# Decoder layer on one core: the second attention's queries and both output projections as three fp32r products, and the feature transposes on halves of 64 rows

## The reference

```
x = x + attn(layernorm(x))            # 16 heads of 16: softmax features of k and q (64 per head), then a linear attention
x = x + xattn(layernorm(x), ctx)      # 8 heads of 32 over 77 context rows of width 192
x = x + ffn(layernorm(x))             # 8 causal heads of 64, values and outputs by one of 8 experts per head and token

xattn:  q = x @ Wq + bq ; w = softmax(q k^T / sqrt(32)) ; out = (w v) @ Wo + bo
attn:   ... num/den per head ... ; out = ctx @ Wo.T + bo
```

## Time and profile before

| what | value |
|---|---|
| median of 3 runs | 913.57 us (910.67 to 914.4) |
| the profiled execution | 910.57 us, its span 907.6 us |
| granted PE clock | 0.998 of full speed over the span |
| PE busy | 853.4 us (94%) |
| DVE busy | 609.5 us (67%) |
| ACT busy | 310.1 us (34%) |
| POOL busy | 319.6 us (35%) |

### The profile page before, as it was taken

One profiled execution on the slowest core, in us unless ns is written; L12 is line 12 of the kernel. 1 busy time (PEld: TensorE's weight loads), 2 busy tenths in 40 slices (PEclk: granted clock), 3 DMA queues, 4 the chain that ended last, 5 costly groups with the idle time before them and its releaser, 6 DMA issues.

```text
span 907.6 us, 17162 instructions
## 1 busy us (share of the span) xinstructions
PE 853.4 (94%) x6944; PEld 648.0 (71%) x6944; DVE 609.5 (67%) x894; ACT 310.1 (34%) x510; POOL 319.6 (35%) x307
## 2 busy tenths in 40 slices
PE   5979899999999998989999888999999999998998
PEld 3657678877756543889976675888777556458998
DVE  4767566566555466888868674765764555687887
ACT  3637655210055554111034475641002444440000
POOL 5213312221457888367520032200004745771000
PEclk9999999999999999999999999999999999999999
DMA  8104000424224553255540000012122010316562
GB/s 274 43 26 140 2 1 1 145 74 138 70 70 143 168 193 96 81 190 177 170 139 1 3 3 1 1 55 77 64 92 93 2 26 2 72 45 192 183 193 87
DMA packets 46789, 80.15 MB, mean 88 GB/s; under 512 B 13064, under 2 KB 24104, under 8 KB 46712
## 3 DMA queue, kind: packets, MB, share of 16 engines
q1 hardware_dynamic: 46711, 79.07, 28.3%
HBM read 59.55 MB, written 19.33 MB: 87 GB/s over the span
## 4 chain that ended last, share of the span: by engine, by line
PE 81%; POOL 6%; DVE 5%; ACT 3%; DMA 3%; issue 2%; SPq 0%; POOLq 0%; DVEq 0%; ACTq 0%
PE ps L1238 19%; PE ps L1643 11%; PE ps L1565 6%; PE ps L1649 5%; PE ps L1476 5%; PE ps L1537 5%; PE ps L1246 5%; POOL xT L610 4%; PE ps L1423 3%; PE ps L1500 3%; PE ps L1380 3%; PE ps L1397 3%; PE ps L1280 2%; PE ps L1317 2%; PE ps L1438 2%
## 5 line engine op out<-in xcount | busy, mean ns | idle before, releaser
L610 POOL TENSOR_TENSOR xT<-xT,region 128x1024 f32<-128x1024 f32 (+5 forms) x80 | 129.7, 1622 | 71.1 <-PE ps L1565 65.9
L1643 PE MATMUL ps<-expert_hi,k_hi 128*128 128x256 f32 x512 | 124.6, 283 | 4.6 <-DVE k_hi L1137 4.6
L1153 DVE COPY_PREDICATED region<-region,ps 128x512 f32<-128x512 uint32 x112 | 82.3, 735 | 66.7 <-PE ps L1238 66.0
L1643 PE MATMUL ps<-expert_lo,k_hi 128*128 128x256 f32 x512 | 123.1, 279 | 0.0
L1077 DVE TENSOR_REDUCE region<-ps 128x2 f32<-128x1024 f32 (+2 forms) x96 | 89.1, 954 | 46.2 <-PE ps L1510 25.3
L1238 PE MATMUL ps<-expert_hi,wide_hi 128*128 128x512 f32 x256 | 102.4, 400 | 0.0
L1643 PEld LDWEIGHTS ps<-expert_hi,k_hi 128*128 128x128 f32 x512 | 96.0, 188 | 6.0 <-issue 4.8
L1238 PE MATMUL ps<-expert_hi,wide_lo 128*128 128x512 f32 x256 | 100.0, 391 | 0.0
L1238 PE MATMUL ps<-expert_lo,wide_hi 128*128 128x512 f32 x256 | 99.8, 390 | 0.0
L1643 PEld LDWEIGHTS ps<-expert_lo,k_hi 128*128 128x128 f32 x512 | 96.7, 189 | 0.0
L1137 DVE TENSOR_TENSOR k_hi<-region 128x1024 fp32r<-128x1024 f32 x64 | 81.9, 1280 | 17.1 <-issue 16.8
(11 more groups left out here) (161 smaller groups left out, 1641.5 us busy)
## 6 DMA issues: line engine op xcount, KB each, us to landing
region<-hot_rows SPq DMA_DIRECT2D x128, 128.0 KB, 3.3
expert_hi<-halves_kept SPq DMA_DIRECT2D x22, 384.0 KB, 3.3
expert_lo<-halves_kept SPq DMA_DIRECT2D x22, 384.0 KB, 4.3
halves_kept<-expert_hi SPq DMA_DIRECT2D x16, 512.0 KB, 5.4
halves_kept<-expert_lo SPq DMA_DIRECT2D x16, 512.0 KB, 6.2
expert<-in_value_experts SPq DMA_DIRECT2D x8, 512.0 KB, 4.6
expert<-in_output_experts SPq DMA_DIRECT2D x8, 512.0 KB, 4.4
gb<-scale_rows SPq DMA_DIRECT2D x16, 256.0 KB, 4.0
```

The costliest lines, as they stand in the source:

```text
L610: pool.tensor_tensor(acc(c)[:, heads, lo:CH], acc(c)[:, heads, lo:CH], PT[:, k % RING, heads, lo:CH], ALU.add).then_inc(sem["added"], 1)
L1153: dve.copy_predicated(V3[:, t].rearrange("p (h k) -> p h k", k=HD3), chosen.unsqueeze(2).broadcast_to([P, H3, HD3]), ps[:, n % 4, :].rearr ...
L1643: mm(ps[:, 4 + t // 2, t % 2 * D:(t % 2 + 1) * D], k_hi[n % 2][:, t * P:(t + 1) * P], w[:, slot, columns], start=(n == 0 and t % 2 == 0 an ...
```

## The change

- **Splits of the weights.** In the key stage of each batch, ACT rounds the three weights WoT, W2q and W2o to their high halves (after the exponentials of tiles 2, 3 and 5), and POOL subtracts to get the low halves, ahead of the maximum over the partitions. The halves lie in buffers of the feed-forward stage that are free until then (q_hi, k_hi, k_lo).
- **Output projections.** ACT's copy of `cx` transposed now writes the high half `cxT_hi`. DVE subtracts it from PSUM for the low half `cxT_low`, as its first work of each step, and PE makes y from six fp32r products instead of two fp32 ones. What waited for ACT's copy of bank 4 (`cxT_sb`) now waits for `cxT_low`: y, the next transpose of `cx`, and `sums_turned`, which writes to bank 4 as well.
- **Queries.** The normalised rows of a = 0 go to `wide_hi` (by ACT) and `wide_lo` (by DVE, `row_low`) and no longer to `xT`, and each of the four query products per batch is six fp32r products of 512 columns instead of two in fp32. `row_low` stands near the start of the step after the tile was transposed, for the last tile of each four at the end of the same step.
- **Feature transposes.** Each block of 128 x 128 is transposed as two halves of 64 tokens, on the upper and on the lower 64 rows of PE, into two different banks. ACT's copies put them back in order.

The diff, cut to its core:

```diff
@@ -179,6 +178,10 @@
                                   for n in ("k_hi", "k_lo", "q_hi", "q_lo"))
+        W2q_hl, WoT_hl, W2o_hl = (w[0][:, :].rearrange("p (w a n) -> p w a n", w=2, a=DA) for w in (q_hi, k_hi, k_lo))
+        cxT_hi, cxT_lo = (k_hi[1][:, i * 2 * D:(i + 1) * 2 * D].rearrange("p (i a s) -> p i a s", i=2, a=DA)
+                          for i in range(2))
+        SPLITS = ((W2q, W2q_hl), (WoT, WoT_hl), (W2o, W2o_hl))
         o_lo = lambda p: (wide_hi, wide_lo)[p // 2][:, p % 2, :]
...
@@ -267,6 +270,7 @@
         QUERIES_AT = {3: (0,), 4: (1,), 7: (2, 3)}
+        SPLIT_AT = {2: 0, 3: 1, 5: 2}
         OFFSET = (0, 10)
@@ -569,6 +573,10 @@
                         pool.wait_ge(w3_lo, i + 1)
+                for i, (w, halved) in enumerate(SPLITS):
+                    until(pool, "split_hi", b, i + 1)
+                    pool.tensor_tensor(halved[:, 1], w[:, :, :], halved[:, 0].bitcast(fp32),
+                                       ALU.subtract).then_inc(sem["split_lo"], 1)
                 until(pool, "ak_top_ready", b, 1)
@@ -644,6 +652,10 @@
                 until(act, "xnT_ps", b, a * TT + t + 1)
+                if a == 1:
+                    copy(wide_hi[:, :, t * P:(t + 1) * P],
+                         ps[:, row_bank(b, a, t), 0:D].rearrange("p (a s) -> p a s", a=DA), "xT_ready")
+                    return
@@ -702,6 +714,13 @@
                     act.activation(E1[:, t, :], E1[:, t, :], ACT.Exp).then_inc(sem["e_ready"], 1)
+                    if t in SPLIT_AT:
+                        w, halved = SPLITS[SPLIT_AT[t]]
+                        if b == 0:
+                            act.wait_ge(later_in, 16 * LOADS_LATER)
+                        else:
+                            until(act, "mo_used", b - 1, NEP)
+                        copy(halved[:, 0], w[:, :, :], "split_hi")
                     for n in queries[1:]:
@@ -741,11 +760,13 @@
                         i = t % 2
+                        turned = phT[:, i, :].rearrange("p (k i s) -> p i k s", i=2, s=HALF)
+                        halves = ps[:, 0:2, :].rearrange("p i (k s) -> p i k s", s=HALF)
                         if a == 0:
-                            copy(phT[:, i, :], ps[:, 0:2, :].rearrange("p a s -> p (a s)"), "fT_sb")
+                            copy(turned, halves, "fT_sb")
                         else:
-                            act.activation(phT[:, i, 0:CH], ps[:, 0, :], ACT.Copy)
-                            copy(phT[0:K2L, i, CH:CH + P], ps[0:K2L, 1, 0:P], "fT_sb")
+                            act.activation(turned[:, :, 0:K2C - 1], halves[:, :, 0:K2C - 1], ACT.Copy)
+                            copy(turned[0:K2L, :, K2C - 1], halves[0:K2L, :, K2C - 1], "fT_sb")
                     for a, t in due(s, 0):
@@ -753,7 +774,7 @@
                             until(act, "y_ps", b, a * TT + t - 1)
-                        copy(cxT[:, t % 2, :, :], ps[:, 4, 0:D].rearrange("p (a s) -> p a s", a=DA), "cxT_sb")
+                        copy(cxT_hi[:, t % 2], ps[:, 4, 0:D].rearrange("p (a s) -> p a s", a=DA), "cxT_sb")
                     for a, t in due(s, 6):
@@ -973,12 +994,27 @@
                                       ALU.mult).then_inc(sem["wv_ready"], 1)
+                def row_low(t):
+
+                    cs = slice(t * P, (t + 1) * P)
+                    until(dve, "xT_ready", b, TT + t + 1)
+                    dve.tensor_tensor(wide_lo[:, :, cs],
+                                      ps[:, row_bank(b, 1, t), 0:D].rearrange("p (a s) -> p a s", a=DA),
+                                      wide_hi[:, :, cs].bitcast(fp32), ALU.subtract).then_inc(sem["x_lo"], 1)
+
...
                 for s in range(LAST):
+                    for a, t in due(s, 4):
+                        until(dve, "cxT_sb", b, a * TT + t + 1)
+                        dve.tensor_tensor(cxT_lo[:, t % 2], ps[:, 4, 0:D].rearrange("p (a s) -> p a s", a=DA),
+                                          cxT_hi[:, t % 2].bitcast(fp32), ALU.subtract).then_inc(sem["cxT_low"], 1)
+                    for a, t in due(s, 7):
+                        if a == 0 and t % TC < TC - 1:
+                            row_low(t)
@@ -1046,6 +1082,9 @@
                                           ALU.mult).then_inc(sem["cx_ready"], 1)
+                    for a, t in due(s, 6):
+                        if a == 0 and t % TC == TC - 1:
+                            row_low(t)
                     for a, t in due(s, 7):
@@ -1213,6 +1252,8 @@
                 until(pe, "xT_ready", b, idx if b + a else idx - 1)
+                if idx > TT:
+                    until(pe, "x_lo", b, min(idx, 2 * TT) - TT)
                 for h in range(DA):
...
@@ -1246,6 +1287,15 @@
                 last.then_inc(sem[name], 1)
+
+            def cross_queries(n):
+
+                c, half = n // 2, n % 2
+                parts = [(w, x, i) for i in range(DA) for w, x in ((0, wide_hi), (0, wide_lo), (1, wide_hi))]
+                for k, (w, x, i) in enumerate(parts):
+                    last = mm(ps[:, 2 + n % 2, :], W2q_hl[:, w, i, half * P:(half + 1) * P], x[:, i, c * CH:(c + 1) * CH],
+                              start=(k == 0), stop=(k == len(parts) - 1))
+                last.then_inc(sem["q2_ps"], 1)
@@ -1353,8 +1403,8 @@
                         until(pe, "numT_sb", b, t)
-                        until(pe, "cxT_sb", b, t - 1)
-                        until(pe, "xT_ready", b, TT + max(0, t - 4))
+                        until(pe, "cxT_low", b, t - 1)
+                        until(pe, "x_lo", b, max(0, t - 4))
                     for k in range(PAIRS1):
@@ -1394,8 +1444,10 @@
                             r = P if a == 0 else min(P, K2 - k * P)
-                            last = pe.transpose(ps[0:r, k // TC, k % TC * P:(k % TC + 1) * P],
-                                                phi[:, t % 2, k * P:k * P + r], ident)
+                            for i in range(2):
+                                tokens = slice(i * HALF, (i + 1) * HALF)
+                                last = pe.transpose(ps[0:r, i, k * HALF:(k + 1) * HALF],
+                                                    phi[tokens, t % 2, k * P:k * P + r], ident[tokens, tokens])
                         last.then_inc(sem["fT_ps"], 1)
@@ -1416,12 +1468,15 @@
                     for a, t in due(s, 4):
-                        until(pe, "cxT_sb", b, a * TT + t + 1)
+                        until(pe, "cxT_low", b, a * TT + t + 1)
                         if a + t:
                             until(pe, "var_ready", b, (a + 1) * TT + t)
-                        for i in range(DA):
-                            last = mm(ps[:, 7, 0:D], cxT[:, t % 2, i, :], (WoT, W2o)[a][:, i, :],
-                                      start=(i == 0), stop=(i == DA - 1))
+                        else:
+                            until(pe, "split_lo", b, len(SPLITS))
+                        parts = [(x, w, i) for i in range(DA) for x, w in ((cxT_hi, 0), (cxT_hi, 1), (cxT_lo, 0))]
+                        for k, (x, w, i) in enumerate(parts):
+                            last = mm(ps[:, 7, 0:D], x[:, t % 2, i, :], (WoT_hl, W2o_hl)[a][:, w, i, :],
+                                      start=(k == 0), stop=(k == len(parts) - 1))
                         last.then_inc(sem["y_ps"], 1)
@@ -1440,7 +1495,7 @@
                         until(pe, "cx_ready", b, a * TT + t + 1)
-                        until(pe, "cxT_sb", b, a * TT + t)
+                        until(pe, "cxT_low", b, a * TT + t)
                         for h in range(DA):
@@ -1448,12 +1503,12 @@
-                            until(pe, "xT_ready", b, TT + t + 1)
+                            until(pe, "x_lo", b, t + 1)
...
                                     until(pe, "q2_sb", b, n - 1)
-                                projection(n, 2, W2q, "q2_ps")
+                                cross_queries(n)
```

More of the change, by code:

```diff
@@ L147, in decoder_layer @@
         numT = view(CH)
-        at[0] = 5 * 1024
+        at[0] = 5 * 1024 + 512
         cx = view(2 * D).rearrange("p (i n) -> p i n", i=2)
-        cxT = view(2 * DA * P).rearrange("p (i a s) -> p i a s", i=2, a=DA)
         phT = view(2 * H1 * NF).rearrange("p (i n) -> p i n", i=2)
@@ L203, in decoder_layer @@
             f_ps=2 * TT, top_ready=2 * TT * DA, f_sub=2 * TT, f_exp=2 * TT, fT_ps=2 * TT, fT_sb=2 * TT,
-            num_ps=2 * TT, cx_ready=2 * TT, cxT_ps=2 * TT, cxT_sb=2 * TT, y_ps=2 * TT,
+            num_ps=2 * TT, cx_ready=2 * TT, cxT_ps=2 * TT, cxT_sb=2 * TT, cxT_low=2 * TT, split_hi=3, split_lo=3, y_ps=2 * TT,
             q2_ps=2 * NC, q2_sb=2 * NC,
@@ L213, in decoder_layer @@
             mo_hi_ready=NEP, mo_lo_ready=NEP,
-            x_lo=TT, piece_hi=2 * E3, piece_lo=2 * E3, mo_used=NEP, bank_full=TC - 1, out_ready=TC,
+            x_lo=2 * TT, piece_hi=2 * E3, piece_lo=2 * E3, mo_used=NEP, bank_full=TC - 1, out_ready=TC,
         )
@@ L1228, in values @@
                 if e == 0:
-                    until(pe, "x_lo", b, t + 1)
```

(1 more changed line is left out.)

## The result

The changed kernel took 925.03 us (median of 4 runs, 922.7 to 926.3) and the kernel before, measured beside it, 912.18 us: a ratio of 1.0132, 95% interval 1.0106 to 1.0157. The change makes the kernel 12.9 us slower, where the forecast had 3.3. Its profiled execution took 924.73 us with a span of 922.9.

A forecast was written before the change was run, and what follows sets the result against it. PE bounds the kernel with DVE close behind; the change makes DVE set full steps, so PE's savings mostly become idle time. Step terms sum to 1.65 us per batch, twice +3.3: 913.57 + 3.3, say 917 us, range 906 to 927.

The forecast's parts named there:

- PE's 21 us: PE's total saving, were it alone: output projections 5.4, queries 3.5 and feature transposes 12 us.
- PE's terms: PE's savings by part: 0.17 us per output projection, 0.9 per query pair, about 0.4 or 0.35 per tile's transposes.
- The rival of row halves that do not overlap: Feature transposes: halves load one after the other, full steps lengthen, about 6 us per batch, 929 us; chance 0.10.
- the 15 to 20 I had named as a sign: Profile after: PE's busy time would fall by about 15 to 20 us while its span does not.
- DVE's term: DVE's 48 new low-half subtractions would cost 0.34 us each, 16.3 us in all.
- steps 5 to 7: First attention's full steps: DVE needs 4.55 us a step, PE's savings become idle time, +0.5 us per batch.
- 14 to 17: Second attention's full steps: DVE-bound at 3.54 us against 3.58 or 3.8 before, -0.3 us per batch.
- The weights' splits are hidden: Key stage, ahead of POOL's maximum over partitions: splits cost 0, with up to 2.6 us in batch 0 kept in the range.
- Steps 10 to 13: Around the second queries: low operations add to DVE and delay the queries, shorter queries give 0.9 back, +0.2 us per batch.
- Steps 8 and 9: After the first attention's features: `sums_turned` and queries wait for DVE, queries 0.9 shorter, +0.8 us per batch.
- the tail: Steps 18 to 21: y waits for ACT's copy and DVE's subtraction, partly given back, +0.45 us per batch.
- handoffs cost more: The added ACT, DVE, PE link is exposed at 0.3 us in some 14 further steps per batch: 925 us; chance 0.20.

The follow-up runs named there:

- e8: Changed kernel, weight splits behind the reduction, DVE's 24 low operations a batch left out and high halves read in their place: 903.56 us, 0.9898 of before.
- e15: Changed kernel, weight splits behind the reduction, low halves made but neither awaited nor read by the products: 913.10 us, 1.0024 of before.
- e11: The kernel before, unchanged, profiled a second time: span 913.5 us, 5.9 us longer than in its first profile.
- e7: Kernel before with row halves only, and ACT's second copy of the ffn key weights one exponential earlier: 904.88 us, 0.9923 of before.
- e2: Kernel before with the weight splits added ahead of the reduction and used for nothing: 916.80 us, 1.0067 of before.
- e1: Changed kernel with POOL's three weight-split subtractions moved behind the reduction over partitions: 920.21 us, 1.0106 of before.
- e3: Kernel before with only the feature transposes done on row halves: 907.61 us, 0.9964 of before.
- e5: Kernel before with row halves and the queries as products of halves, their weight split behind the reduction: 912.41 us, 1.0006 of before.
- e9: Changed kernel, splits behind the reduction, low operations moved from DVE to POOL, reading ACT's second copies: 965.77 us, 1.0606 of before.
- e13: Changed kernel, splits behind the reduction, low operations on POOL, ahead of its norm step: 926.49 us, 1.0152 of before.

## Why the prediction was wrong

- **What bounds the kernel** was right: DVE takes over, clearly so in the first attention, and PE's 21 us do not come through. e8 shows what they are worth with DVE free: 9 us.
- **PE's terms** were right in the main: half transposes 0.64 per 16 (forecast 0.48 plus 0.15). The rival of row halves that do not overlap fell. By the Trainium skill's page "TensorE: Matmul & The Clock Gate" (Part 2, LDWEIGHTS), whose rule is for one load, 16 loads in a row would have taken 1.7, an estimate from the page; the traces say 0.04 us for each. Two savings were over-sized: y takes 0.82, not 0.70, and the two queries 3.07 in e15, not 2.85. By starts PE saves some 15 us, an estimate from the steps of both traces. Its busy time fell by 4.7 alone, not by the 15 to 20 I had named as a sign. That sign was weak: the two profiles of before differ by 4.8 themselves (853.4 and 858.2). That half clock and the modelled ends of short products fill the gap is likely and not shown.
- **DVE's term** of 0.34 an operation was right (0.33). The steps 5 to 7 came at +0.12/+0.58 for +0.5 (0.50 of batch 1's also stands in e11), and 14 to 17 at -0.64 for -0.3.
- **The step that failed most was "The weights' splits are hidden".** I took 0 and kept 2.6, for operations that last longer. They did not, yet the first batch lost 2.7: the amount was in the range, by luck, for its reason was wrong. The row had it: 6.58 us of "issue" ahead of the reduction, of which I took 2.3 to be a delay of its own behind the maxima and the rest to be free. None was free: e7, whose last operation ended 3.8 us earlier, started the reduction 0.2 us behind its maxima and not 2.3. In batch 1, where I said "POOL has nothing else before", DVE's first maxima behind it moved by 1.9 against the last ones ahead of it. Sum 4.6 us by the traces, 6 by e2's times, where 0 stood.
- **Steps 10 to 13** added 0.2, where +1.28 a batch was measured at full clock (1.47 to s3, then -0.19). The terms as written, 0.9 on DVE, 0.45 for `row_low` and 0.9 given back, make 0.45 and not 0.2. The 0.9 came out as 1.47: the sum took off the 0.29 for which DVE had idled ahead of step 13, and in its place stands a wait for ACT's copy ahead of `row_low`, as DVE's timeline after the change has it. And the queries gave back 0.65, not 0.9 (3.07 for 3.72).

```profile
119.33 0.42 DVE L1001 TENSOR_TENSOR wide_lo<-ps,wide_hi 128x256 fp32r<-128x256 f32 x1 [0.48 <-ACT wide_hi L641]
```

- **Steps 8 and 9 and the tail** were undersized: 1.3 for 0.8, and 1.03 for 0.45. e15 shows that the products' wait is half of the first (0.65) and all of the second. Half of the miss at the queries is again their smaller saving.
- **Half clock** was in no term: 1.46 at the second queries of batch 1, and a part, not separable, of the 0.75 and 2.88 us from f0 to f4. e11 has 0.69 and 0.95 there without the change.

Together: 4.6 + 2 x (0.5 + 1.1 + 0.6 - 0.15 - 0.35) + 5.1 = 13.1 above the forecast's 3.3, so 16.4; the spans differ by 15.3, the stretches outside the attentions by -1. The times differ by 12.9. The first profile of before, to which all this is compared, took 910.57 us, under all of its timed runs, at a granted clock of 0.998; e11 had 0.993. The rival "handoffs cost more" gave 925 and the time is 925.03. That is in part luck: it took its 8 us from a link exposed at 0.3 in some 14 further steps a batch; the traces have it at both queries and in the tail alone, and e15 puts it at 7.5 us with the half clock in it. The rest of the miss is the splits' place, which no rival named, at 2.4 (e1) to 6 us (e2), and DVE's larger terms.

What stays open: how much of DVE's 11.5 us is the wait of `sums_turned` for bank 4 to be read twice. To take that wait away needs another bank, of which there is none free; it was not tried. Why before has no half clock at 66 to 69 us, where e1, e3, e5 to e9, e13 and e15 have it, was not settled either.

## What to carry to other kernels

An idle engine ahead of an awaited operation is not free time until the profile names what it waits for: put nothing new ahead of a reduction over partitions on POOL, and end POOL's ordinary work 7 us before the reduction's data come. When a change takes work from the bound and gives it to an engine at 90%, price each new link at every place where the chain crosses it, and take an engine's idle time off its bill only where a row shows that the new work can fill it. Split a change into its parts early: here one part (row halves, with a copy moved by one tile) is 0.8% faster than before, and the other two lost it.

## What the runs showed of the hardware

- A reduction over partitions on POOL started no earlier than 5.6 to 6.8 us after POOL's last ordinary operation, in every run, and the first ordinary operation behind it came 7.4 us after it in e1 (51.82 + 0.39 to 59.58), 6.7 in batch 1.
- A pair of 64-row transposes of 64 columns on the two row halves costs 0.08 us, where one of 128 rows cost 0.11 to 0.13.
- From f7 on, the segments between landmarks repeat within 0.04 us over profiles and batches of a kernel at the same clock (s0 to s3: 7.94 or 7.95 in before, 9.40 or 9.41 in after, e1 and e15), so a shift of 0.1 us there can be read from one profile, though run times scatter by 0.3%. From f0 to f7 this does not hold: with no half clock in batch 0 of either profile of before, f0 to f4 took 19.67 and 20.36.
